# First attention's key blocks: expert inputs turned four at a time, base products laid as single matmuls, second couple two matmuls later

## The reference, cut to what matters

```
xn = layernorm(x)
q, k, v = xn @ Wqk.T + b, xn @ Wv.T + b          # 8 heads of 8 numbers
s = softmax(q @ k.T) / 8 @ v ; s = s @ Wo.T + bo
logits = xn @ W_router.T ; combine = top-2 softmax weights over 8 experts
base = xn @ W_base.T + b_base                    # 1024x512 @ 512x512
expert = ((xn @ A[e].T) * combine[e]) @ B[e].T * 2, summed over e
x = x + s * silu(base + expert)
```

## Time and profile before

| what | us |
|---|---|
| median of three runs | 1482.02 |
| profiled execution | 1485.61 |
| its span, first to last instruction | 1483.8 |
| TensorE busy | 1392.6 (94%) |
| VectorE busy | 985.2 (66%) |
| ScalarE busy | 855.7 (58%) |
| GpSimd busy | 633.9 (43%) |
| key blocks, first couple to last PV | 80.4 to 219.3 |

### The profile page before, as it was taken

The page is one execution under the profiler, slowest core; times in us unless marked ns, Lnnn a source line. Parts: engine busy times, 40 slices in busy tenths (PEclk is TensorE's granted clock), DMA queues, the critical chain, the costliest instruction groups (busy, mean ns, idle before and its releaser), DMA issues.

```text
span 1483.8 us, 21377 instructions
## 1 busy us (share of the span) xinstructions
PE 1392.6 (94%) x7358; PEld 1087.5 (73%) x7358; DVE 985.2 (66%) x1851; ACT 855.7 (58%) x2103; POOL 633.9 (43%) x966
## 2 busy tenths in 40 slices
PE   4989988799999999999999999999999999989997
PEld 3733336588778888878887788888778887768786
DVE  6666644476787777777776777776786777775233
ACT  3345572465766666666766666666766666563211
POOL 4322353444454435545443445444554445433311
PEclk9989996899999999999999999999999999999999
DMA  4100021010020101011010201110020111023010
GB/s 139 64 1 1 1 94 59 15 30 30 29 73 2 58 20 54 21 39 59 15 41 19 73 20 39 42 31 30 30 72 1 44 34 38 28 66 133 15 58 28
DMA packets 35883, 61.02 MB, mean 41 GB/s; under 512 B 9056, under 2 KB 13280, under 8 KB 35776
## 3 DMA queue, kind: packets, MB, share of 16 engines
q1 hardware_dynamic: 35776, 59.66, 12.6%
HBM read 49.68 MB, written 9.96 MB: 40 GB/s over the span
## 4 chain that ended last, share of the span: by engine, by line
PE 66%; DVE 8%; issue 6%; ACT 2%; POOL 1%; DMA 0%; POOLq 0%; DVEq 0%; SPq 0%
PE T L2239 7%; PE T L1870 7%; PE T L1872 6%; PE T L1871 6%; PE S L1872 4%; PE S L1871 4%; PE S L1870 4%; PE WB L1870 4%; PE WB L1871 4%; PE WB L1872 4%; PE VB L1872 4%; PE VB L1870 4%; PE VB L1871 4%; PE T L2132 2%; DVE R L1648 2%
## 5 line engine op out<-in xcount | busy, mean ns | idle before, releaser
L848 POOL TENSOR_TENSOR RI<-SM,C 128x1 f32<-128x1 f32 x256 | 143.1, 559 | 503.7 <-ACT PB L1184 502.7
L1641 DVE CUSTOM_DVE_ANT_0 PB<-S,REL,SLC 128x128 f32<-128x128 f32 (+7 forms) x256 | 204.4, 813 | 82.3 <-PE S L1872 80.8
L1184 ACT ACTIVATE PB<-PB,NM 128x128 f32<-128x128 f32 (+7 forms) x256 | 198.9, 777 | 69.6 <-DVE NM L1641 63.5
L1249 ACT ACTIVATE R<-T 128x512 fp32r<-128x512 f32 x288 | 170.8, 594 | 100.7 <-PE T L2239 98.8
L849 POOL TENSOR_SCALAR PB<-PB,RI 128x128 f32<-128x128 f32 (+7 forms) x256 | 215.0, 840 | 25.2
L1648 DVE TENSOR_TENSOR R<-T,R 128x512 fp32r<-128x512 f32 x288 | 197.4, 688 | 42.3 <-ACT R L1249 23.8
L2239 PE MATMUL T<-C,PB 128*128 128x128 f32 x1152 | 176.6, 276 | 12.3 <-DVE R L1648 7.1
L2239 PEld LDWEIGHTS T<-C,PB 128*128 128x128 f32 x1152 | 134.1, 140 | 48.4 <-DVE R L1648 18.5
L1163 ACT ACTIVATE JUNK<-WB 128x128 bf16<-128x128 f32 x256 | 67.4, 278 | 95.2 <-PE WB L1872 95.2
L1870 PE MATMUL WB<-R,XT 128*128 128x512 f32 x288 | 117.5, 408 | 2.7 <-ACT G L1141 2.7
L1871 PE MATMUL WB<-R,XT 128*128 128x512 f32 x288 | 114.2, 397 | 0.0
(11 more groups left out here) (275 smaller groups left out, 3512.7 us busy)
## 6 DMA issues: line engine op xcount, KB each, us to landing
RAW<-w SPq DMA_DIRECT2D x86, 256.0 KB, 2.8
DQ<-codes SPq DMA_DIRECT2D x16, 352.0 KB, 3.5
DQ<-absmax SPq DMA_DIRECT2D x16, 352.0 KB, 3.0
dequantised<-DQ SPq DMA_DIRECT2D x16, 352.0 KB, 2.2
PB<-x SPq DMA_DIRECT2D x12, 256.0 KB, 3.3
PB<-dequantised SPq DMA_DIRECT2D x5, 512.0 KB, 4.4
PB<-x_scratch SPq DMA_DIRECT2D x8, 256.0 KB, 3.5
out<-PB SPq DMA_DIRECT2D x8, 256.0 KB, 2.0
```

Source lines behind the costliest of these rows:

```text
L848: ch.link(e.tensor_tensor(RI[:, k:k + 1], SM[:, k:k + 1], C[:, C_EXP + 5:C_EXP + 6], ALU.pow))
L1184: e.activation(pb(m, a, 0, L), pb(m, a, 0, L), ACT.Exp, scale=-1.0, bias=NM[:, k:k + 1], accum_out=SM[:, k:k + 1]).then_inc(exp_done, 1)
L1249: e.activation(r(PT + AT[i, ("PV", kb)] % 3 * 1024, 512), T[AT[known, it] % 2][:, :], ACT.Copy).then_inc(t_act, 1)
L1641: e.tensor_tensor_reduce(out=pb(m, a, 0, L), in0=bank[:, 0:L], in1=REL[:, TOK - L:TOK], scale=SLC[:, a:a + 1], scalar=3.0e38, op0=ALU.add, ...
```

## The change

1. **Experts' inputs turned four tiles at a time.** X g turns four tiles (512 columns). X 0 stands ahead of block 0, X 1 in block 1. Their split halves get 1024 columns each at OT, so `high_on` moves its buffer from OT + 512 to PT + 1024.
2. **Base products as single matmuls.** B t m is now one matmul, m = 0 to 11. Five stand in each of two blocks, the last two and HN t in the third; in a block, two stand ahead of ST 1 and the rest behind it. HN t ends in block 3t, HN 7 in block 21.
3. **Couples.** None ahead of block 0 any more. In block 0 ST 1 follows ST 0 directly, then a couple, HN 0 and a couple. Blocks 1 and 2 hold three couples each, blocks 3 to 22 two. The second one follows ST 1, with two single base matmuls between PV and ST 1.
4. **One block earlier.** `FILL_X = 22`, `EARLY_X = 23`: the output items start in block 23, and XT 3 comes in block 31, no longer in the tail.
5. WB's uses are counted by one table for F, WO and PQ.

```diff
-W_AT = {("F", t): t for t in range(NT)}
-FILL = [("X", 0), ("HN", 0)]
+EARLY = 4
+W_AT = {}
+for _x in ([("F", t) for t in range(NT)] + [("WO", t) for t in range(NT)] + [("PQ", 0), ("PQ", 1)]):
+    W_AT[_x] = len(W_AT)
+FILL_X = 22
+FILL = {0: [("HN", 0)]}
 for _t in range(1, NT):
-    FILL += [("B", _t, 0), ("B", _t, 1), ("X", _t), ("B", _t, 2), ("B", _t, 3), ("HN", _t)]
-FILL_X = 24
+    _b = [("B", _t, m) for m in range(3 * KT)]
+    FILL.update({3 * _t - 2: _b[:5], 3 * _t - 1: _b[5:10], 3 * _t: _b[10:] + [("HN", _t)]})
-PAIRS_PRE = 2
-def pair(n):
-    return ("MM", 1 + n // PAIRS, n % PAIRS)
+def couples(x):
+    if x <= 6:
+        u, even, odd = 1, {0: 0, 1: 1}.get(x, x + 1), {0: 0}.get(x, x if x < 3 else x + 1)
+    else:
+        u, even, odd = x // NT + 1 + (x % NT == 7), (x + 1) % NT, (x + 1) % NT
+    extra = {1: ("MM", 1, 4), 2: ("MM", 1, 7)}.get(x)
+    return ("MM", u, 2 * even), ("MM", u, 2 * odd + 1), extra
-EARLY, EARLY_X = 4, 24
+EARLY_X = 23
 def unit_items(x):
-    maxima = [[pair(2 * x + PAIRS_PRE + i)] if 2 * x + PAIRS_PRE + i < 3 * PAIRS else [] for i in range(2)]
-    a, b = (min(n, FILL_X) * len(FILL) // FILL_X for n in (x, x + 1))
-    fill = FILL[a:b] + head_items(x - EARLY_X)
-    seq = [("ST", 0)] + maxima[0]
-    if x:
-        seq.append(("PV", x - 1))
+    fill = FILL.get(x, []) + head_items(x - EARLY_X)
+    first, second, extra = couples(x) if x < 23 else (None, None, None)
+    if x == 0:
+        return [("ST", 0), ("ST", 1), first] + fill + [second]
+    seq = [("ST", 0)] + ([first] if first else []) + [("PV", x - 1)]
+    if x == 1:
+        seq.append(("X", 1))
     if x in (7, 15, 23):
         seq.append(("SH", x // NT + 1))
-    return seq + [("ST", 1)] + maxima[1] + fill
+    cut_ = 2 if second else 0
+    return seq + fill[:cut_] + [("ST", 1)] + ([second] if second else []) + fill[cut_:] + ([extra] if extra else [])
...
-                    elif it[0] == "B" and it[2] == 2:
+                    elif it[0] == "B" and it[2] == 4:
                         tanh0(it[1] - 1)
...
+            def base_part(t, m):
+                if m == 0:
+                    pe.wait_ge(w_free, W_AT["F", t])
+                kt, c = m // 3, m // 3 * 512
+                e.matmul(WB[:, :], xt(m % 3 // 2, kt, t * P, P), r((WBASE_H, WBASE_L, WBASE_H)[m % 3] + c, D),
+                         start=m == 0, stop=False)
...
-            def turn_hn(t):
-                k = M_AT["X", t]
+            def turn_hn(g):
+                k = M_AT["X", g]
                 mring(k)
-                pe.wait_ge(hn_ready, t + 1)
-                e.transpose(T[k % 2][:, 0:P], HN[:, t * P:(t + 1) * P], IDENT).then_inc(m_full, 1)
+                pe.wait_ge(hn_ready, 4 * g + 4)
+                for t in range(4):
+                    last = e.transpose(T[k % 2][:, t * P:(t + 1) * P], HN[:, (4 * g + t) * P:(4 * g + t + 1) * P], IDENT)
+                last.then_inc(m_full, 1)
```

More of the change, by code:

```diff
@@ L136, in unit_items @@
 def unit_items(x):
[L138 to L143 removed]
+    fill = FILL.get(x, []) + head_items(x - EARLY_X)
[5 more added lines that the diff above has]
+        seq.append(("X", 1))
     if x in (7, 15, 23):
         seq.append(("SH", x // NT + 1))
[L146 removed]
+    cut_ = 2 if second else 0
+    return seq + fill[:cut_] + [("ST", 1)] + ([second] if second else []) + fill[cut_:] + ([extra] if extra else [])
 M_AT = {("SH", 0): 0}
+PRELUDE = [("X", 0)]
 _k = 1
[L151 removed]
+for _i in PRELUDE + [i for x in range(NBX) for i in unit_items(x)]:
     if _i[0] in ("MM", "SH", "X", "OS", "OH", "XT"):
@@ L272, in tail_items @@
 def tail_items(k):
-    seq = [("XT", EARLY - 1)] if k == 0 else []
+    seq = []
     seq += token_items(EARLY + k, EARLY, NT)
@@ L290 @@
 S_BASE = S_PRO + 4
-W_OUT = NT
-W_PRO = W_OUT + NT
-W_BASE = W_PRO + 2
+W_BASE = len(W_AT)
 PV_BASE = UNITS * NT
@@ L728, in load_codes @@
                     else:
-                        sp.wait_ge(w_free, W_OUT + NT)
+                        sp.wait_ge(w_free, W_AT["WO", NT - 1] + 1)
                     sp.dma_start(CODES, codes[cc * P:(cc + 1) * P, :]).then_inc(in_codes, 16)
@@ L937, in add_x @@
             def add_x(t):
-                hold(pool, w_free, W_OUT + t + 1, p_passed)
+                hold(pool, w_free, W_AT["WO", t] + 1, p_passed)
                 hold(pool, in_x[t % 4], 16 * (t // 4 + 3), p_passed)
@@ L1127, in high_on @@
                 if t >= 2:
-                    act.wait_ge(w_full, W_OUT + t - 1)
-                e.activation(r(OT + 512 + t % 2 * 256, P), T[k % 2][:, 0:P], ACT.Copy).then_inc(high, 1)
+                    act.wait_ge(w_full, W_AT["WO", t - 2] + 1)
+                e.activation(r(PT + 1024 + t % 2 * 256, P), T[k % 2][:, 0:P], ACT.Copy).then_inc(high, 1)
+            high_hn(0)
             for x in range(NBX):
@@ L1198, in _ @@
                     elif kind == "PQ":
-                        sum_squares(b, W_PRO + b + 1, None)
+                        sum_squares(b, W_AT[x] + 1, None)
                     elif kind == "KV":
@@ L1547, in low_on @@
                 if t >= 2:
-                    dve.wait_ge(w_full, W_OUT + t - 1)
-                o = OT + 512 + t % 2 * 256
+                    dve.wait_ge(w_full, W_AT["WO", t - 2] + 1)
+                o = PT + 1024 + t % 2 * 256
                 e.scalar_tensor_tensor(r(o + P, P), rf(o, P), C[:, C_MASK + 3:C_MASK + 4], T[k % 2][:, 0:P],
@@ L1556, in gated_output @@
                 dve.wait_ge(gate_done, t + 1)
-                dve.wait_ge(w_full, W_OUT + t + 1)
+                dve.wait_ge(w_full, W_AT["WO", t] + 1)
                 g = G[:, t * D:(t + 1) * D]
@@ L1578, in _ @@
             add_shift(0)
-            for n in range(PAIRS_PRE):
-                max1(*pair(n)[1:])
+            low_hn(0)
             for x in range(NBX):
@@ L1668, in scale_q0 @@
                 scale_qk(m, m + 1, None)
-                dve.wait_ge(w_free, W_PRO + m + 1)
+                dve.wait_ge(w_free, W_AT["PQ", m] + 1)
                 dve.sem_inc(qk_ready, 1)
@@ L2056, in output0 @@
             def output0(t, low, count):
-                pe.wait_ge(w_free, W_OUT + t)
+                pe.wait_ge(w_free, W_AT["WO", t])
                 if t == 0:
@@ L2069, in _ @@
             turn_shift(0)
-            for n in range(PAIRS_PRE):
-                max1(*pair(n)[1:])
+            turn_hn(0)
             for x in range(NBX):
@@ L2084, in _ @@
                     elif it[0] == "B":
-                        base(it[1], it[2])
+                        base_part(it[1], it[2])
                     elif it[0] == "HN":
@@ L2157, in _ @@
                 if kind == "PQ":
-                    project_q(block_of(b), W_PRO + b, lambda kt: C_PRO["Q", 0, kt])
+                    project_q(block_of(b), W_AT[x], lambda kt: C_PRO["Q", 0, kt])
                 elif kind == "WO":
@@ L2162, in _ @@
                     k = T_AT[x]
-                    if kind in ("OS", "OH", "XT"):
+                    if kind in ("OS", "OH", "XT") or k < T_OUT + 2:
                         ring0(k)
```

28 lines of the change are left out of this document (13 added, 15 removed).

## The result

The changed kernel takes 1490.01 us (median of 12 runs, 1488.21 to 1500.89), beside 1483.55 us for the kernel before in the same runs. The ratio is **1.0048, 95% interval 1.0025 to 1.0072**: some 7 us slower. The forecast was 1480 us and a small gain. The time lies inside the range of 1468 to 1491 and within the 1%, but on the other side of no change. Medians here are over all executions, while the ratios leave out those more than 1.5% above the fastest of their kernel (one of e8_gate_start, two each of e10_and_busy_wait and e11_and_start_busy).

The account below looks back on a forecast made before the run. TensorE, busy for 94% of the span, was taken as the bound; 5.6 - 0.9 - 1.2 + 0.4 + 1.0 = 4.9 us gained, 1.4 with the clock loss in full. Taking 2.0 from 1482.02 gave 1480 us, range 1468 to 1491.

Parts of the forecast that it names:

- The clock after the stall: Output items behind the last turned shift: 1.2 GHz for 10.6 us, two blocks, about 3.5 us lost, bounds 0 and 17.
- rival B: Lower clock stays from block 23 to 31, blocks lacking base products: 17 us lost against 4.9 gained, 1494 us; chance 0.12.
- A new block of 3.99 us: Key blocks: 2.09 from first couple to second plus 1.90 to the next first one, 3.99 us per block.
- blocks 3 to 21: These 19 blocks together: 77.9 us against 83.5, so 5.6 gained, of which 2.9 is the stretch at 1.2 GHz.
- No loss by the split base runs beyond the 2.09: Key blocks: cutting a base run pays its edges twice; 2.09 us between couples includes it, the other half's wait covers it.
- The start, 0.9 lost: Ahead of block 3: nine couples with X 0 and X 1; block 3 at 100.0 for 99.09, between -1 and +2.5.
- The new wait: Blocks 22 and 23: last shift queued on GpSimd behind bias and gates, TensorE idle 3.8 us, 1.2 us lost for the pair.
- Blocks 24 to 31, 0.4 gained: Output blocks and the tail's start: same items, one fewer (OS 0), 29.4 us becomes 29.0.
- XT 3's wait of 1.00 gone: Tail: XT 3 leaves it, and with it the wait before the tail's second turn, 1.0 us gained.
- Rival A: No stall at the last shift: 1.2 lost becomes 2 gained, no clock drop, 8.0 us gained, 1474 us; chance 0.12.
- Rival C: Tail keeps the full clock: about 9 us gained on top of 4.9, 1468 us; chance 0.12.

Follow-up runs that it names:

- e8_gate_start: Changed kernel with GpSimd's last gate behind block 22's items and the couples of the start as before the change: 1474.75 us, 0.994 of the kernel before.
- e10_and_busy_wait: e9 plus five unread matmuls of 512 columns ahead of the last turned shift: 1472.12 us, 0.9917 of the kernel before.
- e11_and_start_busy: e9 plus three unread matmuls behind each of the first four couples, last wait left open: 1464.93 us, 0.9855 of the kernel before.
- e3_busy_wait: Changed kernel with 14 unread matmuls of 512 columns filling TensorE's wait ahead of the last turned shift: 1482.78 us, 0.9964 of the kernel before.
- e1_gate_behind: Changed kernel with GpSimd's last gate moved behind block 22's items, so the last shift is not queued behind it: 1477.52 us, 0.9945 of the kernel before.
- e4_base_behind: Changed kernel with all base matmuls behind ST 1, none between PV and ST 1: 1489.51 us, 1.0065 of the kernel before.
- e5_wide_behind: Changed kernel with six unread matmuls of 512 columns behind ST 1 of block 23: 1485.7 us, 0.9993 of the kernel before.
- e2_stall_before: Kernel before with only a stall added, three GpSimd additions of 512 columns ahead of the last shift: 1488.93 us, 1.0024 of the kernel before.
- e9: Changed kernel with last gate behind block 22's items, one base matmul between PV and ST 1, start's couples as before: 1469.24 us, 0.99 of the kernel before.
- e7: Changed kernel with last gate behind block 22's items and one base matmul between PV and ST 1: 1473.66 us, 0.993 of the kernel before.
- e6: Changed kernel with last gate behind block 22's items and no base matmul between PV and ST 1: 1480.67 us, 0.9966 of the kernel before.
- e13_all_busy: e9 plus three unread matmuls behind each of the first four couples and five ahead of the last turned shift: 1464.84 us, 0.9875.

## Why the prediction was wrong, point by point

- **The clock after the stall, about 3.5 lost**: this is the step that failed. That the clock would fall was right; how long it stays low was taken from the start of the key blocks, 10.6 us. The first low stretch was 11 us (189 to 200), but a second one came at 210 to 230, and from block 24 to the last PV the kernel lost 10.1 us where the terms gave 3.1. By e3_busy_wait, which fills the wait, the lower clock behind it is worth about 12 us of time, and by the line of the result's section the lower mean clock cost 9.5. How much of the second stretch hangs on the wait stays open, as e1_gate_behind has a shorter one at the same PV without it (3 us: 30.06 for 27). The price of a full stretch was right: rival B's 17 us appear in e4_base_behind (45.07 for 27.06, 18.0). B's mechanism, that no wide matmul stands behind the wait, was the larger part (e5_wide_behind gives back 8 of some 12 us), and I gave it 0.12 although the same part had named the moved products.
- **A new block of 3.99 us**: right. 4.01 was measured. But blocks 3 to 21 gained 3.9 us and not 5.6: they took 78.9 for a forecast of 77.9, and from couple to couple 82.7 before, where the forecast had counted 83.5 from ST to ST.
- **No loss by the split base runs beyond the 2.09**: right. With no split a block takes 3.76, so the two matmuls cost 0.25 per block, as 2.09 + 1.90 against twice 1.88 says. The Trainium skill (TensorEngine Tiling (Array Packing), Key Properties) says that a change of tiling mode drains the engine. The trace agrees: the two base matmuls between PV and ST took 0.66 (133.52 to 134.18), where 2 x 0.23 is 0.46.
- **The start, 0.9 lost**: mis-sized, 2.6 measured (102.44 for 99.85; forecast 100.0). The forecast set a couple against the ST of block 3 (99.09), and the couple itself came at 99.85 before, so that only 0.15 was forecast between like marks. The steps were priced at 1.5 us for the lower clock. The clock was down at 84 to 90, 94 to 101 and 104 to 107, and from the couple ahead of X 1 to the next lie 5.12 (85.65 to 90.77), where 3.5 were reckoned. One profile says little here: in e2_stall_before, whose start is that of the kernel before, the ninth couple came at 102.14, and with the new start it lies between 102.44 and 104.67 in eight profiles.
- **The new wait**: right in place, cause and size: 3.46 for 3.8. That the queue of GpSimd was not in the list, and that a number (`FILL_X`) moved it past the last couple, could be read in the code alone.
- **Blocks 24 to 31, 0.4 gained**: not found. At full clock (e3_busy_wait) they take 27.7 from the ST of block 24 to the last PV, for 27.5 before.
- **XT 3's wait of 1.00 gone**: right. A wait of 0.81 for ScalarE stands there instead, but from the last PV to the tail's first projection matmul the full-clock profile of e1_gate_behind takes 3.59 (222.93 to 226.52) where the kernel before took 4.53.
- **Rival A** (no stall) is near in time when the gate is mended, 1474 for a measured 1477.5, but by luck: it worked out 8.0 us gained, most of it ahead of the output items, and in that profile block 24 starts 1.3 us later than before the change (192.11 for 190.77).
- **Rival C** (the tail keeps the full clock, about 9 us) has its size in that same profile: the tail took 22.31 us there for 31.70, 9.4 less, and as little in four others. What keeps the tail nearly free of the lower clock in one execution and not in another, no run shows.

So the forecast missed in two terms of one sign. Ahead of block 24 3.5 us of gain did not come, and behind it the lower clock cost some 7 us more than its term; the tail gave 2.6 back. Without the clock the forecast was 4.9 us gained; by the line of the result's section, an estimate, it was 2.5.

The Trainium skill (TensorE: Matmul & The Clock Gate, Why this matters for your kernels) warns of idle gaps of TensorE between bursts of matmuls, behind which the clock is down. The traces agree: all five profiles with an idle wait of 3.3 us or more at this place show the fall. By that rule the forecast would have been 1.4 gained, and I took 2.0.

## What to carry to other kernels

When an item is moved by one number, walk every engine's list and look for work that hangs on the number but not on the list; a cheap producer behind two long instructions costs all that they last. A wait of TensorE of some 3 us has to be priced with what stands behind it: with wide matmuls behind it, it cost here little more than itself (e2_stall_before), without them several times itself. Where such a wait can't be removed, unread wide matmuls in it or behind it may pay for themselves, as they did here in e3_busy_wait and e5_wide_behind. And where executions of one kernel differ by more than the edit is worth, set the mean granted clock beside each time before a profile is read: the profiled execution may be one of the rare ones.

## What the runs showed of the hardware

- A wait of 3.3 to 3.9 us in five kernels (3.46, 3.31, 3.46, 3.88, 3.46) was followed each time by matmuls at 1.2 GHz. Waits of 0.98 to 0.99 at the same place were not, in three profiles. Behind 1.20 and 1.22 (e9, e11) PV took 1.93 us some 2 us later; behind 1.24 (e7) nothing fell until 205 us; behind 1.47 (e6) the turned shift itself took 1.09.
- TensorE can be listed as busy all through and stay at the lower clock. In the changed kernel it was busy for 20.72 of 21.00 us, with output items only, and granted 0.51:

```profile
209.50:230.50 21.00, 20.72 (x76) 6.69 (x74) 9.99 (x16) 11.54 (x15) 7.44 (x10) 0.51 0.30 93
```

- In e5_wide_behind six matmuls of 128 x 128 x 512 in 2.86 us were the last ahead of a rise. But the clock also rose with output items alone, in the changed kernel at about 200 us and in e1_gate_behind at 216.
- The clock can fall with no wait over 1 us ahead of it: in e13_all_busy at about 193.8, and in others at 199 to 210. What decides it from one execution to the next stays open, and with it a spread of 8 to 33 us between the executions of one kernel that ran twelve times.
